# Token scatter of a mixture-of-experts layer split over two DRAM tables, its GpSimd program written out without loops, and the correction of the attention prologue moved to GpSimd

## The reference, cut to what matters

```
...
x = layernorm(x + attention0(x))      # 16 heads of 8; mean and mean |s| of a row's scores; powers of 4
x = layernorm(x + experts0(x))        # 16 experts, each takes its 256 best tokens
x = layernorm(x + attention1(x))      # softmax attention
x = layernorm(x + experts1(x))        # 8 experts, every token through its best 2
...
# experts0:
scores = softmax(flat_x @ gate_w.T).T
topk_weight, topk_idx = top_k(scores, C)          # C = 256
xg = flat_x[topk_idx]
h = gelu(xg @ Wg) * (xg @ Wu);  eo = (h @ Wd) * topk_weight
flat_out = zeros.at[topk_idx].add(eo)
out = flat_out + shared(x)
...
```

## Time and profile before

| | us |
|---|---|
| median of the runs shown | 1144.07 (1141.48, 1144.07, 1144.14) |
| the profiled execution, whole | 1145.06 |
| its span, first to last instruction | 1143.3 |
| busy in the span: PE, DVE, ACT, POOL | 966.1, 750.8, 554.8, 352.7 |

### The profile page before, as it was taken

How to read it: one execution, slowest core, us unless ns; L and a number is a source line. 1 busy time by engine, 2 the same in 40 slices (tenths; PEclk the granted TensorE clock), 3 DMA queues, 4 the chain that set the end, 5 groups by cost and what they waited for, 6 DMA issues and landing times.

```text
span 1143.3 us, 18275 instructions
## 1 busy us (share of the span) xinstructions
PE 966.1 (84%) x6011; PEld 474.3 (41%) x6011; DVE 750.8 (66%) x1543; ACT 554.8 (49%) x615; POOL 352.7 (31%) x785
## 2 busy tenths in 40 slices
PE   5699999999997764797817889999999888999996
PEld 3222223222324533686704333333333245566664
DVE  5879999999996585333334977777778116544446
ACT  2488889888985212221205024555555763222222
POOL 3053355335535000777632013333333430000000
PEclk8599999999998695899956559999999997999998
DMA  3401101110103011365433230222201100000001
GB/s 133 148 1 43 43 1 42 41 41 0 41 2 119 16 47 22 96 167 128 84 56 141 93 118 19 78 86 85 62 24 42 44 29 1 14 14 28 14 14 37
DMA packets 45655, 63.27 MB, mean 55 GB/s; under 512 B 7720, under 2 KB 33672, under 8 KB 42120
## 3 DMA queue, kind: packets, MB, share of 16 engines
q1 hardware_dynamic: 39968, 58.11, 16.3%
q0 software_dynamic: 5632, 4.46, 2.6%
HBM read 50.69 MB, written 11.86 MB: 55 GB/s over the span
## 4 chain that ended last, share of the span: by engine, by line
PE 55%; DVE 23%; issue 9%; ACT 4%; POOL 4%; DMA 4%; DVEq 0%; SPq 0%; POOLq 0%; ACTq 0%
PE causal_ps L1135 10%; PE acc_ps L748 8%; DVE mx L498 6%; PE acc_ps L1042 6%; PE tail_ps L988 5%; PE tail_ps L1145 5%; DVE R L1430 4%; PE causal_ps L1025 3%; DVE tails L1436 3%; PE causal_ps L710 2%; PE causal_ps L721 2%; DMA moe_rows<-out_e,idx_out 2%; ACT EX L1318 2%; POOL moe_rows L1989 2%; POOL G L1973 1%
## 5 line engine op out<-in xcount | busy, mean ns | idle before, releaser
L1318 ACT ACTIVATE EX<-causal_ps 128x1024 f32<-128x1024 f32 (+1 forms) x160 | 146.9, 939 | 156.0 <-PE causal_ps L1025 154.4
L498 DVE TENSOR_REDUCE mx<-tail_ps 128x1 f32<-128x512 f32 x266 | 157.4, 633 | 39.7 <-PE tail_ps L991 21.4
L1205 ACT ACTIVATE R<-R 128x2048 f32<-128x2048 f32 (+1 forms) x80 | 134.7, 1737 | 0.5 <-DVE R L1430 0.5
L1135 PE MATMUL causal_ps<-XT,w 128*128 128x512 f32 x256 | 117.3, 606 | 2.6 <-DVE hid_f L1808 1.9
L988 PE MATMUL tail_ps<-KM,QM 72*128 72x512 bf16 (+1 forms) x320 | 104.5, 355 | 8.8 <-DVE mx L498 3.0
L1025 PE MATMUL causal_ps<-QE,KE 75*128 75x512 bf16 (+3 forms) x384 | 102.2, 337 | 8.5 <-ACT EX L1318 3.1
L1354 ACT ACTIVATE act_f<-causal_ps 128x512 f32<-128x512 f32 x64 | 38.2, 597 | 130.0 <-PE causal_ps L1135 130.0
L1212 ACT ACTIVATE R<-R 128x1792 f32<-128x1792 f32 (+4 forms) x80 | 100.4, 1268 | 0.0
L1430 DVE TENSOR_SCALAR R<-causal_ps 128x1024 f32<-128x1024 f32 (+1 forms) x88 | 93.9, 1070 | 9.7 <-PE causal_ps L710 8.6
L1436 DVE TENSOR_REDUCE tails<-causal_ps 128x1 f32<-128x768 f32 (+4 forms) x96 | 92.8, 967 | 10.6 <-PE causal_ps L721 9.9
L2049 POOL TENSOR_TENSOR pacer<-eps_ln 128x1 f32<-128x1 f32 x160 | 31.2, 195 | 206.9 <-ACT EX L1318 206.2
(11 more groups left out here) (266 smaller groups left out, 1615.0 us busy)
## 6 DMA issues: line engine op xcount, KB each, us to landing
QS<-q_parts SPq DMA_DIRECT2D x8, 576.0 KB
KS<-k_parts SPq DMA_DIRECT2D x24, 192.0 KB
QM<-q_parts SPq DMA_DIRECT2D x8, 576.0 KB
KM<-k_parts SPq DMA_DIRECT2D x24, 192.0 KB
QE<-q_parts SPq DMA_DIRECT2D x8, 576.0 KB
KE<-k_parts SPq DMA_DIRECT2D x24, 192.0 KB
wg<-in_wg_t SPq DMA_DIRECT2D x16, 256.0 KB
wu<-in_wu_t SPq DMA_DIRECT2D x16, 256.0 KB
```

Source lines behind the costliest of these rows:

```text
L498: return reduce(mx[:, par, hh, o0:o0 + step * (cnt - 1) + 1:step], scores[:, 0:cnt * w].rearrange("p (c w) -> p c w", w=w), AX.X, op, **how)
L1135: mm = pe.matmul(banks[2 * ring + o], w[:, k, m * P:(m + 1) * P], XT[:, n * BANK:(n + 1) * BANK], start=True, stop=True)
L1205: act.activation(R4[:, rp, h0:h0 + 2, 0:width], R1[:, rp, h0:h0 + 2, 0:width], ACT.Square).then_inc(squared, 1)
L1318: act.activation(EX[:, rp, hh, 0:width], causal_ps[hh % 2][:, 0:width], ACT.Exp, scale=float(D) ** -0.5).then_inc(exp_done, 1)
```

## The change

1. A second DRAM table. Even experts accumulate into moe_rows[0], odd ones into moe_rows[1], which starts as zeros. Each table has its own semaphore, so scatter e waits for scatter e - 2 only. out_e has four buffers; DVE waits for the scatter of expert e - 4. GpSimd clears Z near the start, SP stores it as the zeros. At the end both tables are read (eight loads in place of four) and DVE adds them chunk by chunk.
2. GpSimd's part of experts0 is written out for all 16 experts. The DMAs read idx directly; the copies and carry_waits are gone. Five gathers run ahead before the first scatter; then gather e + 5, scatter e.
3. Prologue: proj and the rests have places of their own, both in R4, so R1 is free and the rests need not wait for PE's correction. The sums of later keys and k_heads move to GpSimd, as a chain of seven steps on one column each and one multiplication for each sequence; `later` goes. PE makes both corrections after all projections; DVE copies them to corr inside the first quad, at its second step. The bias is added to X on GpSimd between the first and the second quad.

```diff
-        moe_rows = dram("moe_rows", [B * T, P], F32)
+        moe_rows = [dram(f"moe_rows{i}", [B * T, P], F32) for i in range(2)]
...
-        proj = R1[:, :, :, :].rearrange("p a h t -> p (a h t)").rearrange("p (m t) -> p m t", t=T)
+        proj, rests0 = R4[:, 1, :, :], R4[:, 0, :, :]
...
-        out_e = sb("out_e", [P, 2, NH, P], F32, M)
+        out_e = sb("out_e", [P, 4, NH, P], F32, M)
+        Z_odd = sb("Z_odd", [P, NT, P], F32, N)
...
 # SP
+            sp.wait_ge(zeros_set, 1)
+            sp.dma_start(moe_rows[1].rearrange("(i p) d -> p i d", p=P), Z[:, :, :]).then_inc(zeros_out, 16)
...
-            sp.wait_ge(scattered, 16 * NH * E0)
+            for i in range(2):
+                sp.wait_ge(scattered[i], 16 * NH * E0 // 2)
             for n in range(CH):
-                sp.dma_start(Z[:, n * CT:(n + 1) * CT, :],
-                             moe_rows[n * BANK:(n + 1) * BANK, :].rearrange("(i p) d -> p i d", p=P)).then_inc(z_in[n], 16)
+                for z, rows in zip((Z, Z_odd), moe_rows):
+                    sp.dma_start(z[:, n * CT:(n + 1) * CT, :],
+                                 rows[n * BANK:(n + 1) * BANK, :].rearrange("(i p) d -> p i d", p=P)).then_inc(z_in[n], 16)
...
 # PE, prologue: out of the loop over b, behind all projections
+            for b in range(B):
+                pe.wait_ge(corr_ready, b + 1)
+                for i in range(KT - 1):
+                    mm = pe.matmul(acc_ps[:, b * BANK + i * H:b * BANK + (i + 1) * H],
+                                   proj[:, 2 * b, i * P:(i + 1) * P], k_heads[:, b, i, :], start=True, stop=True)
+                mm.then_inc(corr_full, 1)
...
 # ACT
             act.wait_ge(part_done, 2 * REP * B)
+            act.wait_ge(corr_full, B)
             quad(0, 0, first=True)
...
 # DVE, prologue
-                dve.wait_ge(rest_done, 2 * REP * b + 2)
-                link(dve.tensor_reduce(k_tiles[:, b, :], k.rearrange("p (i t) -> p i t", t=P), AX.X, ALU.add))
-                dve.wait_ge(upto_ready, 6)
-                link(dve.tensor_tensor(k_later[:, :, :], later[:, :, :],
-                                       k_tiles[:, b, :].unsqueeze(1).broadcast_to([P, KT - 1, KT]), ALU.mult))
-                link(dve.tensor_reduce(k_after[:, :], k_later[:, :, :], AX.X, ALU.add))
...
-                dve.wait_ge(corr_full, b + 1)
-                take_rests(0, b, proj)
+                take_rests(0, b, rests0, proj)
...
+                dve.tensor_reduce(k_tiles[:, b, :], k.rearrange("p (i t) -> p i t", t=P), AX.X, ALU.add
+                                  ).then_inc(key_sums, 1)
+            def take_corr():
+                dve.wait_ge(corr_full, B)
...
+                    if j == STEP_AT[1] and first:
+                        take_corr()
...
 # DVE, experts0 and what follows
-                if k >= 2 or not isinstance(j, int) or j > 0:
-                    dve.wait_ge(scattered, 16 * NH * (4 * j + k - 1))
+                if not isinstance(j, int) or j > 0:
+                    dve.wait_ge(scattered[k % 2], 16 * NH * (2 * j + k // 2 - 1))
...
+            def both_rows(n):
+                dve.wait_ge(z_in[n], 16 * 2)
+                chunk = slice(n * CT, (n + 1) * CT)
+                dve.tensor_tensor(Z[:, chunk, :], Z[:, chunk, :], Z_odd[:, chunk, :], ALU.add).then_inc(z_summed, 1)
+                dve.wait_ge(z_summed, n + 1)
+
+            layer_norm(1, both_rows)
...
 # POOL, prologue
+            def sum_later_keys(b):
+
+                pool.wait_ge(key_sums, b + 1)
+                pool.tensor_copy(k_after[:, b, KT - 2:KT - 1], k_tiles[:, b, KT - 1:KT]).then_inc(key_step, 1)
+                for i in range(KT - 3, -1, -1):
+                    pool.wait_ge(key_step, (KT - 1) * b + KT - 2 - i)
+                    pool.tensor_tensor(k_after[:, b, i:i + 1], k_after[:, b, i + 1:i + 2], k_tiles[:, b, i + 1:i + 2], ALU.add
+                                       ).then_inc(key_step, 1)
+                pool.wait_ge(key_step, (KT - 1) * (b + 1))
+                pool.tensor_tensor(k_heads[:, b, :, :], k_after[:, b, :].unsqueeze(2).broadcast_to([P, KT - 1, H]),
+                                   own_head[:, :].unsqueeze(1).broadcast_to([P, KT - 1, H]), ALU.mult
+                                   ).then_inc(corr_ready, 1)
+
+            pool.memset(Z[:, :, :], 0.0).then_inc(zeros_set, 1)
+            pool.wait_ge(upto_ready, 4)
+            sum_later_keys(0)
+            pool.wait_ge(v_sb, 1)
+            take_v(0, 0)
+            sum_later_keys(1)
+            pool.wait_ge(v_sb, B)
+            quad(0, 0, after=0)
             pool.wait_ge(x_in, 16)
             pool.wait_ge(w_in, 16 * 2)
             pool.tensor_tensor(X[:, :, :], X[:, :, :], YT[:, 0, 0:P].unsqueeze(1).broadcast_to([P, NT, P]),
                                ALU.add).then_inc(res_in, 1)
...
-            quad(0, 0, after=0)
             quad(1, 1, after=1)
...
 # POOL, experts0
-                pool.tensor_copy(idx_in[:, k, :], src).then_inc(idx_ready, 1)
...
-                pool.tensor_copy(idx_out[:, k, :], src).then_inc(idx_ready, 1)
...
-                    pool.wait_ge(scattered, 16 * NH * e)
-                carry_waits()
...
+            def scatter(e):
                 pool.wait_ge(out_sb, e + 1)
+                if e >= 2:
+                    pool.wait_ge(scattered[e % 2], 16 * NH * (e // 2))
                 for h in range(NH):
+                    pool.indirect_dma_start(out=moe_rows[e % 2], in_=out_e[:, e % 4, h, :], in_offset=None,
+                                            out_offset=bass.IndirectOffsetOnAxis(ap=idx[:, e, h:h + 1].bitcast(U32), axis=0),
+                                            compute_op=ALU.add).then_inc(scattered[e % 2], 16)
...
+            pool.wait_ge(zeros_out, 16)
+            gather(4)
+            for e in range(E0):
+                if e + 5 < E0:
+                    gather(e + 5)
+                scatter(e)
```

More of the change, by code:

```diff
@@ L237, in build @@
         k_tiles = sb("k_tiles", [P, B, KT], F32, A)
-        later = sb("later", [P, KT - 1, KT], F32, A)
-        k_later = sb("k_later", [P, KT - 1, KT], F32, A)
-        k_after = sb("k_after", [P, KT - 1], F32, A)
+        k_after = sb("k_after", [P, B, KT - 1], F32, A)
         own_head = sb("own_head", [P, H], F32, A)
@@ L290, in build @@
         own_done = sem("own_done")
+        key_sums = sem("key_sums")
+        key_step = sem("key_step")
         A.close()
@@ L440, in build @@
         out_sb = sem("out_sb")
-        idx_ready = sem("idx_ready")
-        scattered = sem("scattered")
+        scattered = [sem(f"scattered{i}") for i in range(2)]
+        zeros_set = sem("zeros_set")
+        zeros_out = sem("zeros_out")
+        z_summed = sem("z_summed")
         z_in = [sem(f"z_in{n}") for n in range(CH)]
@@ L687, in _ @@
                     mm.then_inc(v_full, 1)
-                    pe.wait_ge(corr_ready, b + 1)
-                    for i in range(KT - 1):
-                        mm = pe.matmul(acc_ps[:, b * BANK + i * H:b * BANK + (i + 1) * H],
-                                       proj[:, 2 * b, i * P:(i + 1) * P], k_heads[:, b, i, :], start=True, stop=True)
-                    mm.then_inc(corr_full, 1)
+            for b in range(B):
[4 more added lines that the diff above has]
+                mm.then_inc(corr_full, 1)
             pe.wait_ge(w_in, 16 * 2)
@@ L1391, in take_rests @@
                         dve.wait_ge(part_done, 2 * REP * (B * layer + b) + 2 * n + m + 1)
-                        dve.tensor_tensor(rest, values[m][:, :] if values and n == 0 else rest, pt[:, m, n, :],
+                        src = (values[m][:, :] if layer else values[:, 2 * b + m, :]) if n == 0 else rest
+                        dve.tensor_tensor(rest, src, pt[:, m, n, :],
                                           ALU.subtract).then_inc(rest_done, 1)
@@ L1526, in residual @@
                 dve.wait_ge(out_full, CH * layer + n + 1)
+                if layer == 0 and n == 0:
+                    dve.wait_ge(zeros_out, 16)
                 dve.tensor_tensor(Z[:, n * CT:(n + 1) * CT, :], X[:, n * CT:(n + 1) * CT, :],
@@ L1977, in scatter, with gather @@
-            def scatter(j, k):
-                e = 4 * j + k
-                src = idx[:, e, :] if isinstance(e, int) else idx[:, bass.ds(e, 1), :].rearrange("p o h -> p (o h)")
-                pool.tensor_copy(idx_out[:, k, :], src).then_inc(idx_ready, 1)
-                pool.wait_ge(idx_ready, 4 + (8 * j if not isinstance(j, int) or j < 3 else 24) + scat_at(j, k))
+            def gather(e):
+                if e >= 4:
+                    pool.wait_ge(g_sb, e - 3)
+                for h in range(NH):
+                    pool.indirect_dma_start(out=G[:, e % 4, h, :], out_offset=None, in_=xs_rows,
+                                            in_offset=bass.IndirectOffsetOnAxis(ap=idx[:, e, h:h + 1].bitcast(U32), axis=0)
+                                            ).then_inc(gathered[e % 4], 16)
@@ L1983, in scatter @@
```

(35 more changed lines are left out.)

51 lines of the change are left out of this document (13 added, 38 removed).

## The result

The changed kernel takes **1115.88 us**, median of four executions (1114.11 to 1118.09), against 1144.11 for the kernel before (1141.48 to 1151.11): ratio **0.9745**, 95% interval 0.9698 to 0.9792. Forecast: 1117. The profiled execution took 1116.36 with a span of 1114.6, against 1143.3: 28.7 us less.

A forecast was written before the change was run, and what follows sets the result against it. It took GpSimd's indirect DMAs and their landings, 456 to 590 us, as the bound, then the prologue's DVE stops. 1145.06 - 4.6 (prologue) - 25.4 (experts) + 2.6 (reading back) = 1117.7 profiled, 1117 median; range 1111 to 1127.

The forecast's parts named there:

- The place: Expert stage, 456 to 590 us: the chain runs over GpSimd's indirect DMAs and landings; the change works there, -25.4 us.
- The period: Experts on GpSimd: two scatters and two gathers with gaps of 0.30 us take 6.4 us a period, before 7.47.
- rival (a): Experts on GpSimd: the gaps between DMAs stay, 7.1 us a period, +8.5 us, 1126 in all; chance 0.15.
- Tail: Last five experts on GpSimd, without gathers: scatters 3.8 us apart, waiting for no landing but the table's partner.
- Rival (b): GpSimd's one DMA queue serialises all scatters and gathers: a gain of 5 us there, 1138 in all; chance 0.08.
- Both arrive almost together: End of the expert stage: GpSimd reaches scatter 15 at 559.1 us, PE and DVE have its out_e at 558.5.
- Last landing: Last scatter: its second DMA lands 3.26 us after its start, by the row; the skill page's estimate was 2.2.
- Reading back: Reading both tables: eight loads for four, DVE binds at 3.1 us a chunk; +2.6 us, bounds +1 and +4.5.
- Prologue: Before first scores: DVE's two stops for the correction go, first scores near 37.6 us; -4.6 us, bounds -6 and -2.
- the 0.4 set aside for clashes: Prologue: 0.4 us allowed for small clashes in putting first scores at some 37.6 us in place of 42.65.
- the collision with the addition to X: Prologue: k_later took 3.32 us beside GpSimd's addition to X, 0.22 without; 3.1 us of DVE's 7.1 us loss.
- (d): Expert stage: TensorE falls to 1.2 GHz, 5.5 us more per expert at that level, up to 1199; chance 0.03.

## Why the prediction was right, point by point

- **The place.** It was read from where the chain runs over landings, and the gain came there. The two undoings show the two halves: one table alone costs 14.1 us up to the last scatter, the copies 9.1. Together 23.2 of the 25.2 of the table above. Neither undoing brings back GpSimd's loop, its order with two scatters side by side, or the two out_e buffers; the other 2.0 us weren't divided among these.
- **The period.** 6.4 forecast, 6.43 measured; the choice of 0.30 for the gaps, and not the 0.48 of the rows then, was right, and so rival (a) fell. The reason given was half right: of the 1.04 us gained a period, 0.65 are the copies and carriers. The argument against (a) put the 0.48 down to the carrier, but with the carrier back and no loop the gap is 0.15. So it went with the loop, as far as these two kernels show.
- **Tail.** 3.8 forecast, 3.72 measured, and no wait for a landing: 555.24 - 470.41 = 84.8 us for all scatters against 84.9. Rival (b) fell with it: from the last scatter's start to its landing it is 5.1 us, yet the scatters start 3.72 apart. DMAs with different semaphores overlap in the one queue.
- **"Both arrive almost together."** This step failed, at no cost. From out_e of expert 0 to that of expert 15 I had 558.5 - 475.7 = 82.8 us; it took 547.54 - 469.52 = 78.0. Of the 4.8 too many, 3.7 are the last step, which has no next expert's products in it (1.8 us, not 5.5), the rest mostly the pace, 5.44 in place of 5.5. So the end hangs on GpSimd alone. The run with one more expert's gathers ahead agrees: its scatters end 2.7 us sooner after scatter 0.
- **Last landing.** 3.26 us, as the row had it, and not the estimate of 2.2 from the Trainium skill's page DMA: Bandwidth & Descriptors (Anatomy of one DMA).
- **Reading back.** +2.65 in the traces for +2.6; leaving the second table out gives 3.5 back. DVE bound at 3.0 a chunk, as forecast. That the sizes agree so closely is in part luck: at the last chunk, where the term was worked out, it is +3.1.
- **Prologue.** This term was too small: -5.9 at the first scores for -5.0, since GpSimd's chain took 2.25 us for 2.8 and the 0.4 set aside for clashes wasn't needed, and -6.1 at the indices for -4.6. The 0.45 that I charged for the copy to corr in the first quad doesn't show: from the first scores to the indices it is 413.2 us before and 413.1 and 413.4 in the changed kernel's two traces. This is where the 1.3 us come from by which the span fell further than the sum. The attribution was off as well: I gave the collision with the addition to X 3.1 us of the gain. It is 4.4. With DVE's stops gone, the subtractions of the rests come under the addition to X in place of k_later, and they suffer more. Rearranging the corrections without moving X would have gained about 1 us (first scores at 42.15 with the old prologue, 41.12 with X early).
- **A shift on the way that isn't the change's.** At DVE's last step ahead of the ranking the lead was 5.1 us, at the indices 6.1. Between them stand PE's ranking products, a line's own rows for before, after, and the changed kernel run again (least, median and most ns of one, first and last start):

```profile
L883 PE MATMUL causal_ps<-same_e,tile_counts x12: 421/421/421, 434.4 to 437.8; 128*128 128x128 f32 x12
```

```profile
L888 PE MATMUL causal_ps<-same_e,tile_counts x12: 275/280/421, 429.3 to 431.9; 128*128 128x128 f32 x12
```

```profile
L888 PE MATMUL causal_ps<-same_e,tile_counts x12: 421/421/421, 428.1 to 431.6; 128*128 128x128 f32 x12
```

  They ran at the lower level before; in the first trace after, the granted clock rose while they ran. In the same kernel's second trace it didn't, and the indices came at 449.6 all the same, against 449.8. So the 0.9 us at this place differ between executions of one kernel and are no part of the gain.
- **(d)** fell: PE ran at 1.00 from 462 us to its last expert. The 8 us ahead of that have 0.52; before the change it is the same, 0.53 from 460 to 467 us, where the earlier trace rows begins. The stretch behind the last expert has 0.62 with PE idle.

## What to carry over

Where updates must land one by one, a second destination pays only for those with nothing else to issue between them; count the landing against what stands between. Moving a GpSimd operation with SBUF operands out from under another engine's can be worth more than the chain that it was moved for, and a clash that one fix removes may only be hiding the next, so try such moves separately. And read the last step of a pipeline apart from its pace: it has no successor's work in it.

## What the hardware showed that I had not expected

- **Clock phases.** Executions of one kernel fall into groups that go with the mean granted clock: 6.4 us apart without the odd table, 8.7 us with the copies (means of the groups). Edits of 2 us can't be told apart from that with four to six executions; their marks in a trace can.
- **A load beside a scatter.** With loads of 1 MB beside it, the last 64 KB accumulating scatter took 4.89 and 5.13 us to land in two kernels, in place of 3.26 and 3.39 in the changed kernel's two traces.
- **ScalarE's stops.** With 18 gathers issued without a rest, ScalarE stood twice for some 4 us, in two kernels; with 14 it didn't, in one. The trace calls what it waited for remote; what that is stays open.

No variant beats the changed kernel by more than the measurement can tell.
